# Mixer steps taken in pairs and a second buffer for the feed-forward step's first sums (one core, fp32 state-space layer)

## The reference

```python
h = rms(x) * norm_w
gate, hBC, dt = split(h @ in_proj_w.T)          # 8192, 10240, 128
hid, B, C = split(silu(conv4(hBC)))             # causal, 4 taps
M = (C @ B.T) * exp(segsum(A * dt))             # in a chunk of 128
Y_diag = M @ (hid * dt)
states = B.T @ (decay * hid * dt)               # per chunk, carried on
Y_off = (C @ prev_states) * exp(A_cs)
y = Y_diag + Y_off + D * hid
yg = y * silu(gate)
out = x + (yg * rsqrt(mean(yg * yg)) * gnorm_w) @ out_proj_w.T
ffn = (silu(x @ Wg.T) * (x @ Wu.T)) @ Wd.T      # int4 weights, scales per 128 inputs
x = x + s * silu(ffn)
```

## Time and profile before

| | before |
|---|---|
| runs | 2008.63, 2010.82, 2013.45; median 2010.82 us |
| profiled execution, its own time | 2008.87 us |
| its span, first to last instruction | 2007.1 us |
| TensorE busy | 1952.2 us, 97% |
| VectorE, ScalarE, GpSimd busy | 1594.6 (79%), 1483.1 (74%), 1230.5 (61%) |
| mean granted TensorE clock | 0.997 |
| DMA, mean over the span | 120 GB/s |

### The profile page before, as it was taken

The page is one execution under the profiler, slowest core; times in us unless marked ns, Lnnn a source line. Parts: engine busy times, 40 slices in busy tenths (PEclk is TensorE's granted clock), DMA queues, the critical chain, the costliest instruction groups (busy, mean ns, idle before and its releaser), DMA issues.

```text
span 2007.1 us, 32870 instructions
## 1 busy us (share of the span) xinstructions
PE 1952.2 (97%) x10906; PEld 1573.0 (78%) x10906; DVE 1594.6 (79%) x2979; ACT 1483.1 (74%) x2986; POOL 1230.5 (61%) x853
## 2 busy tenths in 40 slices
PE   7998999999999999999999999999999999999998
PEld 6564666777888888888888888888888888888877
DVE  7777899857877878878778787878787878787888
ACT  5245866547787878787878787878787878787776
POOL 5644777544656666666656656565666565666666
PEclk9999999999999999999999999999999999999999
DMA  5615332444424343333333333343433333433423
GB/s 202 192 51 148 100 93 85 157 147 134 132 93 132 93 132 107 125 116 124 121 107 119 105 119 109 115 125 112 122 116 109 116 111 113 156 118 107 135 96 122
DMA packets 114473, 241.75 MB, mean 120 GB/s; under 512 B 23681, under 2 KB 24706, under 8 KB 113794
## 3 DMA queue, kind: packets, MB, share of 16 engines
q1 hardware_dynamic: 110466, 227.06, 35.8%
q0 software_dynamic: 3840, 12.59, 2.2%
HBM read 226.75 MB, written 12.85 MB: 119 GB/s over the span
## 4 chain that ended last, share of the span: by engine, by line
PE 76%; DVE 2%; ACT 1%; issue 0%; DVEq 0%; ACTq 0%
PE s_ps L74 13%; PE s_ps L76 13%; PE s_ps L75 13%; PE s_ps L1861 6%; PE s_ps_o L74 6%; PE s_ps_o L76 6%; PE s_ps_o L75 6%; PE s_ps L1827 5%; PE s_ps L1869 4%; PE s_ps L1819 3%; DVE s_cv L2100 1%; PE s_ps L1845 1%; PE s_ps L1805 1%; PE s_ps L1811 0%; DVE s_state L2076 0%
## 5 line engine op out<-in xcount | busy, mean ns | idle before, releaser
L2278 POOL TENSOR_TENSOR w_lo<-w_raw,w_hi 128x1024 fp32r<-128x1024 f32 x142 | 340.0, 2401 | 534.7 <-ACT w_hi L1932 534.7
L74 PE MATMUL s_ps<-h_hi,w_hi 128*128 128x512 f32 x1152 | 463.0, 402 | 6.2 <-DVE s_hid L2105 4.6
L76 PE MATMUL s_ps<-h_hi,w_lo 128*128 128x512 f32 x1152 | 450.2, 391 | 0.0
L75 PE MATMUL s_ps<-h_lo,w_hi 128*128 128x512 f32 x1152 | 448.6, 389 | 0.0
L2100 DVE SCALAR_TENSOR_TENSOR s_cv<-s_ps,s_par,s_cv 128x511 f32<-128x511 f32 (+2 forms) x480 | 355.9, 744 | 15.5 <-ACT s_cv L1975 9.7
L2295 POOL TENSOR_TENSOR s_lm<-s_lm,s_cbt 128x512 f32<-128x512 f32 x256 | 326.8, 1301 | 12.5 <-ACT s_lm L1957 12.5
L1950 ACT ACTIVATE s_lm<-s_rows,s_steps 128x128 f32<-128x128 f32 x1024 | 312.4, 390 | 2.0 <-PE s_ps L1861 2.0
L1975 ACT ACTIVATE s_cv<-s_ps,s_par 128x512 f32<-128x512 f32 x160 | 124.5, 778 | 221.7 <-PE s_ps L76 221.7
L74 PEld LDWEIGHTS s_ps<-h_hi,w_hi 128*128 128x128 f32 x1152 | 216.5, 188 | 53.1 <-DVE s_hid L2105 5.8
L76 PEld LDWEIGHTS s_ps<-h_hi,w_lo 128*128 128x128 f32 x1152 | 216.2, 188 | 47.5
L75 PEld LDWEIGHTS s_ps<-h_lo,w_hi 128*128 128x128 f32 x1152 | 216.9, 188 | 41.0
(11 more groups left out here) (291 smaller groups left out, 4107.5 us busy)
## 6 DMA issues: line engine op xcount, KB each, us to landing
w_raw<-in_w_in SPq DMA_DIRECT2D x144, 512.0 KB, 3.6
s_rows<-acs_dram SPq DMA_DIRECT2D x256, 256.0 KB, 4.3
s_wo_raw<-in_w_out SPq DMA_DIRECT2D x128, 256.0 KB, 3.7
w_raw<-in_gu_q SPq DMA_DIRECT2D x14, 512.0 KB, 3.6
f_d_q<-in_d_q SPq DMA_DIRECT2D x28, 256.0 KB, 2.7
f_d_w<-in_d_s SPq DMA_DIRECT2D x28, 256.0 KB, 3.4
table<-shifted SPq DMA_DIRECT2D x16, 256.0 KB, 2.7
xs<-in_x SPq DMA_DIRECT2D x8, 256.0 KB, 6.1
```

Source lines behind the costliest of these rows:

```text
L74: nc.tensor.matmul(dst, l_hi, r_hi, start=start, stop=False)
L75: nc.tensor.matmul(dst, l_hi, r_lo, start=False, stop=False)
L76: return nc.tensor.matmul(dst, l_lo, r_hi, start=False, stop=stop)
L2278: nc.gpsimd.tensor_tensor(w_lo[:, slot, :], w_raw[:, slot, :], w_hi[:, slot, :].bitcast(F32), ALU.subtract).then_inc(w_lo_ready, 1)
```

## The change

**Feed-forward.** sum_a has two buffers by parity of the step: odd steps use room in a tile that is needed only later. act_group waits for the product of step m-2. A copy into that tile waits for the last product.

**Mixer.** A unit is four double slots s = 0 to 3, each with the pairs a = 2s and b = 2s+1. The four banks are named A to D and every job has one by the list. TensorE's order in a double is OFF a, OFF b, DIAG a, DIAG b, T, G a, H a, (CB or BT), G b, T, H b, ST, ST, (C and B projections), OP a, OP b; the T and ST jobs are two pairs ahead. The first block does T and ST of two pairs ahead, the last unit keeps single slots. The orders of ScalarE, VectorE, GpSimd and SyncE are rewritten to match. The C and B projections move from slot 2 to double 1, behind pair 3. The sum of squares is taken in the same unit (last double): four transposes of the summed squares and one reduction by VectorE instead of four matmuls with a column of ones; the division by the count moves into ScalarE's square root. yoff of odd pairs goes to s_tg, so that two can be there at once.

The diff, cut to its core:

```diff
-        def sum_a(n, part):
+        odd_sums = group[:].rearrange("p g n -> p (g n)")[:, 0:2 * NB * SEQ].rearrange("p (s t) -> p s t", s=2 * NB)
+
+        def sum_a(m, n, part):
+            if m % 2:
+                return odd_sums[:, 2 * n + part, :]
             if (n, part) == (1, 0):
                 return wdt[:].rearrange("p k h -> p (k h)")
...
-                    act.wait_ge(inner_ready[n], m)
+                if k == 0 and m >= 2:
+                    act.wait_ge(inner_ready[n], m - 1)
...
+def first_jobs():
+
+    jobs = []
+    for k in range(KC):
+        if k in (2, 3):
+            jobs += [("T", 1, k - 2)]
+        if k == BC_SLOT:
+            jobs += [("H", 1, C_AT), ("H", 1, B_AT)]
+        if k == 6:
+            jobs += [("BT", 1, 0), ("CB", 1, 0)]
+        if k < KC - 1:
+            jobs += [("G", 1, k), ("H", 1, tile_of(k))]
+    jobs += [("ST", 1, 0), ("ST", 1, 1), ("H", 1, tile_of(KC - 1)), ("G", 1, KC - 1)]
+    return [(i % BANKS, job) for i, job in enumerate(jobs)]
+
+
+A_BANK, B_BANK, C_BANK, D_BANK = range(BANKS)
+
...
+def double_jobs(s):
+
+    a, b = 2 * s, 2 * s + 1
+    jobs = [(C_BANK, ("OFF", 0, a)), (D_BANK, ("OFF", 0, b)), (A_BANK, ("DIAG", 0, a)), (B_BANK, ("DIAG", 0, b)),
+            (C_BANK, ("T", *divmod(a + 2, KC))), (D_BANK, ("G", 1, a)), (A_BANK, ("H", 1, tile_of(a)))]
+    if s == 2:
+        jobs += [(C_BANK, ("CB", 1, 0))]
+    if s == 3:
+        jobs += [(C_BANK, ("BT", 1, 0))]
+    jobs += [(D_BANK, ("G", 1, b)), (C_BANK, ("T", *divmod(b + 2, KC))), (B_BANK, ("H", 1, tile_of(b))),
+             (C_BANK, ("ST", *divmod(a + 2, KC)))]
+    if s == 3:
+        jobs += [(D_BANK, ("SQ", 0, 0)), (None, ("OP", 0, a)), (D_BANK, ("ST", *divmod(b + 2, KC)))]
+    else:
+        jobs += [(D_BANK, ("ST", *divmod(b + 2, KC)))]
+        if s == 1:
+            jobs += [(A_BANK, ("H", 1, C_AT)), (D_BANK, ("H", 1, B_AT))]
+        jobs += [(None, ("OP", 0, a))]
+    return jobs + [(None, ("OP", 0, b))]
+
...
+        EARLY, LATE = (1, 3, 6, 8), (2, 5, 7, NLOAD)
...
         def pe_ssq(pe, v, dst):
 
             pe.wait_ge(ssq_ready, v.at(KC - 1, KC - 2))
-            pe_squares(ssq, dst, True, True).then_inc(ssq_done, 1)
+            for t in range(TB):
+                mm = nc.tensor.transpose(dst[:, t * P:(t + 1) * P], ssq[:, t * P:(t + 1) * P], ident[:])
+            mm.then_inc(ssq_done, 1)
...
+        def act_double(act, un, s):
+            a, b, v = 2 * s, 2 * s + 1, un.ahead(1)
+            (ua, a_on), (ub, b_on) = pair_at(un, a + 2), pair_at(un, b + 2)
+            h_a, h_b = bank(un, ("H", 1, tile_of(a))), bank(un, ("H", 1, tile_of(b)))
+            act_w(act, *load_unit(un, EARLY[s]))
+            act_wo(act, un, a)
+            act_diff(act, ua, 2 * a_on)
+            act_y(act, un, a)
+            act_sq(act, un, a)
+            act_wo(act, un, b)
+            act.wait_ge(y_chain, (un.u * KC + b) * 2 + 2)
+            act_gate(act, v, a, bank(un, ("G", 1, a)))
+            act_y(act, un, b)
+            act_sq(act, un, b)
+            act_diff(act, ua, 2 * a_on + 1)
+            act_tap(act, v, tile_of(a), h_a)
+            if s == 1:
+                act_w(act, v, LOADS.index(("BC", 0)))
+            act_exps(act, ua, a_on)
+            act_gate(act, v, b, bank(un, ("G", 1, b)))
+            if s:
+                act_tanh(act, v, tile_of(a), h_a)
+            act_diff(act, ub, 2 * b_on)
+            act_diff(act, ub, 2 * b_on + 1)
+            act_tap(act, v, tile_of(b), h_b)
+            if not s:
+                act_tanh(act, v, tile_of(a), h_a)
+            act_exps(act, ub, b_on)
+            act_scale(act, ua, a_on)
+            if s == 1:
+                act_tap(act, v, C_AT, bank(un, ("H", 1, C_AT)))
+            else:
+                act_scale(act, ub, b_on)
+            if s == 3:
+                act_rms(act, un)
+            if load_unit(un, LATE[s]):
+                act_w(act, *load_unit(un, LATE[s]))
+            act_tanh(act, v, tile_of(b), h_b)
+            if s == 1:
+                act_scale(act, ub, b_on)
+                act_tap(act, v, B_AT, bank(un, ("H", 1, B_AT)))
+                act_tanh(act, v, C_AT, bank(un, ("H", 1, C_AT)))
+                act_tanh(act, v, B_AT, bank(un, ("H", 1, B_AT)))
+
+        def act_end(act, un):
...
         def dve_ssq(dve, v, src):
             dve.wait_ge(ssq_done, v.at(1, 0))
-            nc.vector.tensor_scalar(meansq[:], src[:, 3 * P:3 * P + TB], 1.0 / CG, 256 * EPS, ALU.mult,
+            nc.vector.tensor_reduce(sumsq[:], src.rearrange("p (t c) -> p t c", t=TB), AX.X,
                                     ALU.add).then_inc(ssq_took, 1)
...
+        def carried(un, k):
+            return tg[:, 0:3 * P] if k % 2 and not un.last else yoff[:]
...
+            dve_yoff(dve, un, a)
+            dve_yoff(dve, un, b)
+            dve_y_skip(dve, un, a)
+            dve_y_carried(dve, un, a)
+            dve_y_gated(dve, un, a)
+            dve_y_skip(dve, un, b)
+            dve_y_carried(dve, un, b)
+            dve_y_lo(dve, un, a)
+            dve_y_gated(dve, un, b)
+            dve_gate(dve, v, a, bank(un, ("G", 1, a)))
+            turn(0)
+            dve_y_lo(dve, un, b)
+            if s == 2:
+                dve_cb(dve, v, bank(un, ("CB", 1, 0)))
+            if s == 3:
+                dve_bt(dve, v, bank(un, ("BT", 1, 0)))
+            if s == 0 and not un.first:
+                dve_out(dve, un.ahead(-1))
+            if s:
+                dve_tile(dve, v, tile_of(a), h[0])
+            turn(1)
+            if s:
+                dve_silu(dve, v, tile_of(a), h[0])
+            dve_gate(dve, v, b, bank(un, ("G", 1, b)))
+            if not s:
+                dve_tile(dve, v, tile_of(a), h[0])
+            state(0)
+            if not s:
+                dve_silu(dve, v, tile_of(a), h[0])
+            if s == 3:
+                dve_ssq(dve, un, bank(un, ("SQ", 0, 0)))
+            state(1)
+            if s == 1:
+                dve_skip(dve, v)
+            dve_tile(dve, v, tile_of(b), h[1])
+            if s == 1:
+                c_bank, b_bank = bank(un, ("H", 1, C_AT)), bank(un, ("H", 1, B_AT))
+                dve_silu(dve, v, tile_of(b), h[1])
+                dve_tile(dve, v, C_AT, c_bank)
+                dve_conv(dve, v, B_AT, b_bank, 1)
+                dve_silu(dve, v, C_AT, c_bank)
+                dve_conv(dve, v, B_AT, b_bank, 2)
+                dve_conv(dve, v, B_AT, b_bank, 3)
+                dve_silu(dve, v, B_AT, b_bank)
+            else:
+                dve_silu(dve, v, tile_of(b), h[1])
+            if un.u == UNITS - NB and s >= 2:
+                dve_total(dve, 1, 2 * s - 4)
```

542 lines of the change are left out of this document (295 added, 247 removed).

## The result

| | before | changed |
|---|---|---|
| runs, median us | 2009.7 (2008.6 to 2013.5, 4 runs) | 2038.0 (2035.5 to 2040.3, 4 runs) |
| ratio | 1 | 1.014, 95% interval 1.0127 to 1.0152 |
| span of the profiled execution | 2007.1 | 2033.7 |

The change makes the kernel 1.4% slower, where 2006 us (1985 to 2030) was forecast. The profiled execution is the fastest of the four; the other three are 2 to 5 us longer. First the windows of the changed kernel, whose columns are those of the earlier trace rows: a piece of the first block, a steady unit, unit 14, and the last unit.

A forecast was written before the change was run, and what follows sets the result against it. TensorE's record density and new waits were taken to bound the mixer. Steady units 0, first block +1.1, unit 0 +1.6, last unit -3.8, feed-forward -3.5 sum to -4.6 on the 2010.8 median: 2006 us, range 1985 to 2030.

The forecast's parts named there:

- The term for B's silu: Double 1 into 2: silu B ends at 29.15, the second OFF wants its bank at 28.35; TensorE waits 0.87 us.
- the term for y_lo: H of pair a: y_lo ends at 6.62, TensorE arrives at 6.61; wait estimated 0.14 us, bounds 0 and 0.4.
- Dense records: Mixer doubles: fewer half-width trips and small-to-big changes save 0.38 us, giving 22.08 us per double without waits.
- Trip 0.34: Small records of a double: one trip into half-width tiles and back costs 0.34 us; the new order saves one.
- Rival D: Small records of a double: the dense run of 48 is too long, 0 to +10 us, 2006 to 2016; chance 0.10.
- Rival C: H of pair a: chain to y_lo longer than 6.62, 0.1 costs 6 us; at 0.3, 2024 us; chance 0.25.
- VectorE late after double 3: Double 0: skip a starts at 26.2 instead of 25.6, so TensorE waits 0.67 us at H.
- The first block: Mixer's first block: 56.6 becomes 57.7 us, +1.1, with new waits of 3.0 at last G and 2.1 at first OFF.
- Unit 0: Mixer's first unit: 95.36 becomes 96.9 us, +1.6; the 0.67 us wait is absent there.
- The last unit: Last mixer unit: first out-projection comes 10.1 us in instead of 13.9, a gain of 3.8 us.
- Feed-forward: Feed-forward stage: two buffers remove TensorE's waits of 2.3 and 2.0 us; -3.5 us taken, bounds -4.3 and 0.
- B, hidden waits: Mixer units: VectorE and ScalarE earlier than added up, 31 us of waits go, 1975 us, half 1990; chance 0.22.

The follow-up runs named there:

- the edges mended: The three edits plus reordered first block, spread-out totals and ScalarE's exponentials behind taps and gate tanh, against the kernel before: 0.9871, 1981.6 us.
- the three edits: Changed kernel with square from y_hi, reordered B chain in double 1 and squares' transposes late, together; against the kernel before: 0.9933.

## Why the prediction was wrong, point by point

The sum had -4.6 and the spans gave +26.6, so 31.2 us were missed: 9.0 in the first block, 16.8 in units 1 to 14, 2.8 in unit 0, 2.1 in the last unit and 0.5 in the feed-forward part. The mechanisms in the sum were right: denser records, and waits at the ends of serial chains. What failed is the size of its waits. The term for B's silu (0.87) came from a list that left out an instruction, the term for y_lo (0.14) was too small, two pairs of totals were not in the sum at all, and the first block's waits were read from VectorE's order alone.

**Dense records: right.** Trip 0.34: measured 0.35 from the lists with one and two trips. A double with no wait: forecast 22.08. Double 1 of the changed kernel takes 27.83 with 24 big records (5.44) and a wait of 0.33 at H: 22.06. Where the waits at H are gone (the square from y_hi) double 1 takes 27.53, which leaves 22.09. Rival D (too long a run of small records) is out: DIAG and DIAG take 1.90, their pairs 0.11 apart to the end.

**The wait for y_lo: the mechanism right, the term too small.** "Estimate 0.14, bounds 0 and 0.4" measured 0.33 (36 big records in 8.59, and 8.26 where the wait is gone): y_lo was 0.03 later and TensorE there 0.05 earlier (6.56 for 6.61). The prediction's 0.06 for the signal and 0.1 for a record without its weights had no row behind them; 0.15 pass ahead of the waiting record and 0.11 behind it over the usual 0.227. A sum whose two sides differ by 0.01 in 6.6 cannot be priced at its centre. In three doubles that is 0.6 us per unit. It is also the prediction's own sign of being wrong, "if H waits much over 0.2 everywhere". Rival C, put at "0.1 costs 6 us", had this right in price, but not in cause: the chain is as long as it had been added up (6.65 for 6.62).

**VectorE late after double 3: right.** Skip a was to start at 3.20 of double 0 and starts at 3.16. 0.67 and 0.14 of wait were forecast; the span is 22.89, 0.83 over 22.06. That the sum fits to 0.02 is in part luck: the run with the squares late takes 0.57 off and leaves 0.26.

**B's silu: the chain failed.** It was forecast to end at 29.15 us of double 1 and ended at 29.85, and the wait was 1.50 instead of 0.87. The list of VectorE's work there left out one instruction, the skip factors, and the run with them moved gives 29.11 and 0.80. Their duration is the second half of the miss: 1.07 there (1065 ns is also the mean of 11 units), and 0.16 in the kernel before and in the first block:

```profile
447.32 0.16 DVE L2231 TENSOR_SCALAR s_skip<-s_par 128x8 f32<-128x8 f32 x1
```

**Units 1 to 14: forecast 0, measured +16.8.** 0.6 from H and 0.6 from OFF, less 0.2 in the small terms, is the 1.0 us of a steady unit. Unit 14 has 2.6 on top, from another thing left out: two totals (additions of output tiles) at the end of double 2 of that unit, both operands in SBUF. VectorE, then GpSimd beside them:

```profile
1945.17 4.21 DVE L1755 TENSOR_TENSOR xs<-xs,s_end_x 128x512 f32<-128x512 f32 x2
1949.31 0.55 DVE L2274 TENSOR_TENSOR s_yoff<-s_ps,s_scale 128x384 f32<-128x384 f32 x1
```

```profile
1943.67 5.16 POOL L2454 TENSOR_TENSOR w_lo<-w_raw,w_hi 128x1024 fp32r<-128x1024 f32 x2 [1.05 <-ACT w_hi L1995]
```

The two take 4.21 us, and yoff behind them is what TensorE waited for (1.4 at T, then 0.9 at H). With the totals spread out unit 14 takes what a steady unit takes.

**The first block: +10.1 for +1.1.** The two waits that were forecast (3.0 and 2.1) are there with 2.8 and 2.0. Not seen were two of some 0.5, a T whose tile is only just projected (2.4), and a G that waits 2.9 for the gate of step 5, whose tanh stands behind the exponentials, the scale and a table load on ScalarE:

```profile
463.13 1.28 ACT L2019 ACT_TABLE_LOAD   x1
...
465.48 1.05 ACT L2027 ACTIVATE s_scale<-s_rows 64x384 f32<-64x384 f32 x2
466.55 0.60 ACT L2050 ACTIVATE s_tg<-s_ps 128x512 f32<-128x512 f32 x1
```

TensorE stood 2.9 us there, from 465.0 to 467.9, and as it went on the granted clock was at its lower level (1.2 GHz), so that a big record took 0.63 instead of 0.39: in the window 462.88 to 475.82 the clock has a mean of 0.87, which is 1.7 us more. The prediction had walked VectorE's order in the first block and not ScalarE's. The unseen waits (6.3) and the clock (1.7), less 0.3 for the two that were shorter than forecast, make 7.7 of the 9.0; the other 1.3 were not traced to a place. The clock's share differs between executions: the first block of the runs with the product in the gate's place and with the skip factors early has the same jobs and took 70.5 us in each profile, with more time at the lower clock.

**Unit 0: the clock.** Unit 0 is 2.8 over the forecast, and 1.0 of it is the steady unit's. Almost all of the rest is in its first double, which takes 24.01. Its window in the changed kernel, and in the run with the skip factors early:

```profile
487.88:511.89 24.01, 24.01 (x136) 20.30 (x137) 17.06 (x33) 16.75 (x38) 11.71 (x9) 0.93 0.34 96
```

```profile
489.18:511.57 22.39, 22.39 (x136) 18.80 (x137) 17.05 (x33) 16.74 (x38) 11.71 (x9) 1.00 0.24 77
```

At the full clock the double takes 22.39, 0.5 less than in a steady unit (0.67 was forecast, since no double 3 precedes it). In the changed kernel the granted clock is 0.93 of full on the mean, at its lower level just behind TensorE's wait of 2.0 for the first OFF, and that is 1.6 us more.

**The last unit** gained 1.7 of 3.8. Its first out-projection starts 12.2 us into the unit, where 13.9 was read before and 10.1 forecast. The other two totals stand at the end of double 3 of unit 14 and took 2.35 there, ahead of yoff, for which TensorE waited 2.7; the prediction had not counted them.

**Feed-forward: right in size (3.0 in the spans and 2.8 in its own run, for 3.5), half wrong in detail.** Of the two waits that were added up only the one of 2.3 went; that the size comes out so near is in part luck.

**The rivals.** B, hidden waits, was not what the change did, and it priced all waits in the units at 31 us. Taking most of them out gains 42, since they were larger than forecast; B's time, 36 us under the kernel before, is not reached even with the edges mended (26 under).

## What to carry to other kernels

Making the binding engine's own work denser by 0.4 us in 22 is worth nothing if it brings the next consumer to within 0.1 us of the end of a serial chain: price such a meeting at the far bound, or take a link out of the chain first. Walk each engine's whole list between the two points of a chain, small instructions included, in the first and last blocks too. The skip factors and the totals, left out here, are short instructions between SBUF tiles, whose duration depends on what GpSimd does beside them.

## What the hardware showed that I had not expected

VectorE's instructions between SBUF tiles, beside a busy GpSimd: y_lo 0.75 becomes 1.6 to 1.9, the skip factors 0.16 become 1.07, and two totals of 512 columns take 4.21. With one operand in PSUM y_lo keeps its time (746 ns on the mean of 88). For y_lo the records of both engines show the exclusion. For the skip factors they do too: they run from 1122.41 to 1123.48 beside the two instructions of this row, which end at 1123.45, and in the first block GpSimd was idle.

```profile
1120.90 2.55 POOL L2471 TENSOR_TENSOR s_lm<-s_lm,s_cbt 128x512 f32<-128x512 f32 x2 [0.81 <-ACT s_lm L2019]
```

They end 0.03 behind a GpSimd instruction in every unit after the first; in the run with the skip factors early they meet a whole one and take 1.31. They have one tensor operand only, so the rule for two SBUF inputs does not cover them, and the rows alone show it; the reciprocal of the same 8 columns, also beside GpSimd, took 0.20 and did not wait. Each of the two totals of unit 14 ends 0.55 behind one of the two GpSimd instructions shown with them (y_lo ended 0.55 behind as well), and a total that meets no GpSimd instruction takes 0.68, in the version with the three edits. So for the totals too the records show it, though no run of their own does.

The prediction had priced VectorE's instructions by their columns alone. By these rows a short one between SBUF tiles must be priced with a whole GpSimd instruction on top, as its upper bound: 1.3 us where GpSimd works on 512 columns, 2.4 where it works on 1024.
